# Gate product of the last four token groups as two pairs by Strassen's algorithm, with down weights prepared ahead of up weights

## The chip, the cores and the metric

The kernel runs on one core of a Trainium2 chip. The core has TensorE (PE, matrix products into PSUM), VectorE (DVE), ScalarE (ACT), GpSimd (POOL) and SyncE (SP), which here issues nearly all DMAs. Each engine works through its own instructions in order, and they meet in semaphores. The metric is the device time of one execution in microseconds (us), the median over several runs.

## The reference, cut to what matters

An attention over a context of 128 tokens adds to x (2 x 2048 tokens, 512 wide). A feed-forward block with simulated quantisation follows:

```python
x = act_qdq(x)                                  # 16 bit, one scale for the whole tensor
up = act_qdq(x @ lpbq_dequant(w_up).T)          # weights: 4 bit in blocks of 32; 512 -> 1536
gate = act_qdq(x @ lpbq_dequant(w_gate).T)
sig = fixed_qdq_u16(jax.nn.sigmoid(gate))
gate = act_qdq(gate * sig)
o = act_qdq(gate * up)
return o @ lpbq_dequant(w_down).T               # 1536 -> 512
# act_qdq(x): scale = max(max|x| / 32767, 1e-12); clip(round(x / scale), -32768, 32767) * scale
```

Each `act_qdq` needs the maximum over all 4096 tokens before its first value can be rounded, so the gate product must be finished, and kept somewhere, before any of it is used.

## The kernel before, in words

The 4096 tokens are eight groups of 512 (`NG`), the 1536 inner columns twelve blocks of 128 in six units of two (`UPG`), so a product has 48 units (`NU`). An integer activation and a weight are each held as the sum of two 16-bit floats, high and low; one product of a 128-block by 512 tokens takes three matmuls (high x high, low x high, high x low) for each of four blocks of the inner dimension. One unit of one group is thus 2 x 4 x 3 = 24 matmuls of 128x128 by 128x512.

The stages, in time: attention and normalisation (to 130 us), gate product (130 to 380), up product (380 to 631), down product (631 to the end).

Gate stage. TensorE (`unit`, `product`, `gate`, L864 to L886) writes two PSUM banks per unit, two units ahead of ScalarE. ScalarE (`take_gate`, L1114 on) copies a unit to one of two buffers `gate_out`, and writes its signs; it may refill a buffer when its DMA has landed (`g_st`). VectorE (`gate_max`, L1474) takes the maximum. SyncE (`park_gate`, L424) stores the unit and its signs in HBM (`gate_park`, `sign_park`), and in groups 0 to 2 turns the integer activations of the next groups by DMA transpose (`turn_half`); VectorE splits them (`split_h`). The last six units (from `STAY` = 42) stay in SBUF.

The up and down weights are prepared beside this. VectorE takes block maxima (`block_max`, `block_scales`), GpSimd an all-reduce over the partitions (`all_max`), VectorE the common power of two (`common_scale`), GpSimd quantises in eight passes of four operations (`quant_weights`, L685), ScalarE and VectorE split them (`natural_hi`, `natural_lo`), and SyncE turns them by DMA transpose. Up weights are done in groups 0 to 4, down weights in groups 4 to 6; the turned down weights are parked in HBM (`wd_d`, L448). SyncE then issues the first reloads of gate tiles (`fetch_gate`) to the shelf, a region of 23 places in SBUF, tiles 6 to 14 of the order of use before the last gate unit is through, and 15 to 22 just after.

Up stage. TensorE (`raise_unit`, L897) has eight banks, four units: unit n + 4 starts when ScalarE has taken unit n (`take_up`, L1150, the eviction L993). ScalarE's program is, for n = 0 to 47: the gate tiles of `steps(n)` (three for every two units: integer L1168, absolute value L1173, sigmoid L1181), then `take_up(n)`. VectorE works on the same tiles (L1518, L1523, L1529) and takes the maximum of the up unit (L1511). `take_up(n)` waits until the store of unit n - 2 has landed (`u_st`), as there are two buffers:

```python
if n < STAY:
    need(act, u_mx, n - 1)
    need(act, u_st[n % 2], 8 * (n - n % 2))
```

SyncE's program is one list in order: the shelf's loads, then for each n the first loads of the bench (16 more places, in the room of the split activations as TensorE gives them back), `park_up(n - 1)`, the stores of products of tiles 23 on (`park_product`) and the reloads into their places (`refill`). Up to eight `fetch_gate` are in flight: load k waits for load k - 8. From unit 33 the products are quantised (`settle`).

Down stage. The up tiles come back, are multiplied and quantised, and are multiplied with `WD` (`first_pass`, `down_whole`, `down_split`, L910 to L977).

## Time and profile before

| | us |
|---|---|
| median of 3 runs | 904.1 (903.08 to 907.88) |
| span of the profiled execution | 898.3 |
| busy in it: PE, DVE, ACT, POOL | 865.5, 651.1, 560.2, 157.4 |
| gate matmuls (L871), busy | 250.5, 1152 matmuls |
| up matmuls (L903), busy | 249.0, 1152 matmuls |
| mean granted TensorE clock | 0.994 |

The profile is one execution recorded on the chip. Its span goes from the first to the last instruction; the measured time also holds what lies around it. A group of instructions stands by its source line, engine and operation, with its busy time and the mean of one, and the idle time of the engine ahead of it with what ended that. Matmuls overlap, so a matmul's mean (381 ns) is longer than the step from one to the next. "SPq" is SyncE's DMA queue; the time there is that of issuing, and the time to landing is given apart. "issue" stands for time in which an engine waited for nothing that the profile shows.

### The profile page before, as it was taken

To read this page: it belongs to the slowest core of one execution; us is meant where nothing else is said; L and a number is where in the kernel's file an instruction comes from. 1 tells how busy PE (TensorE), PEld (TensorE's weight loads), DVE (VectorE), ACT (ScalarE), POOL (GpSimd) and SP (SyncE) were. 2 spreads that over 40 slices of the span, in tenths; PEclk is the share of its full clock that TensorE was granted. 3 is DMA by queue.
4 is the path that set the end of the run, shared out by engine and by line. 5 is a ranking of instruction groups with operands and counts; after the bars stand their busy time and mean duration, and the time that the engine had idled before them with its cause. 6 is when DMAs were issued, how large, how long until landed. Compare 5 with 4: busy or idle time off the path is not lost.

```text
span 898.3 us, 11791 instructions
## 1 busy us (share of the span) xinstructions
PE 865.5 (96%) x4144; PEld 426.7 (47%) x4144; DVE 651.1 (72%) x918; ACT 560.2 (62%) x673; POOL 157.4 (18%) x160
## 2 busy tenths in 40 slices
PE   7999969999999999999999989999799989999998
PEld 5777544444444444444444434444344434444443
DVE  4879883754346243279997859856999997999892
ACT  2378875553553454489997859763789975555430
POOL 0099940089001950000000000000000000000000
PEclk9999989999999999999999999999999999999999
DMA  9822319775369649884339993799998897989872
GB/s 347 332 93 98 128 59 305 205 194 198 140 234 296 206 161 294 322 319 157 132 149 327 363 347 142 251 402 373 374 379 265 276 322 271 386 286 406 317 294 100
DMA packets 107548, 230.20 MB, mean 256 GB/s; under 512 B 47216, under 2 KB 47216, under 8 KB 105328
## 3 DMA queue, kind: packets, MB, share of 16 engines
q1 hardware_dynamic: 106352, 225.48, 70.8%
q10 hardware_dynamic: 1152, 4.19, 1.3%
q8 instruction: 21, 0.34, 0.2%
q14 instruction: 23, 0.19, 0.1%
HBM read 127.40 MB, written 92.27 MB: 245 GB/s over the span
## 4 chain that ended last, share of the span: by engine, by line
PE 66%; DVE 16%; issue 8%; DMA 6%; ACT 3%; SPq 0%; POOL 0%; DVEq 0%; ACTq 0%
PE ps L871 28%; PE ps L948 13%; PE ps L903 10%; PE ps L975 3%; DVE big L1596 3%; PE ps L804 3%; DVE big L1589 3%; PE ps L743 2%; PE ps L818 2%; DVE small L1523 2%; DMA big<-gate_park 2%; DMA product_park<-big 2%; DVE small L1511 2%; DVE big L1518 1%; PE ps L965 1%
## 5 line engine op out<-in xcount | busy, mean ns | idle before, releaser
L993 ACT ACTIVATE big<-ps 128x1024 f32<-128x1024 f32 (+2 forms) x166 | 138.7, 845 | 189.6 <-PE ps L871 102.8
L871 PE MATMUL ps<-big 128*128 (+1 forms) x1152 | 250.5, 381 | 2.3 <-DVE big L1460 2.3
L903 PE MATMUL ps<-big 128*128 (+1 forms) x1152 | 249.0, 379 | 2.3 <-ACT big L993 2.3
L871 PEld LDWEIGHTS ps<-big 128*128 128x128 f16 x1152 | 113.1, 98 | 139.4 <-issue 4.6
L903 PEld LDWEIGHTS ps<-big 128*128 128x128 f16 x1152 | 112.6, 98 | 138.5 <-issue 2.8
L1478 DVE TENSOR_REDUCE small<-big 128x1 f32<-128x1024 f32 x48 | 58.3, 1219 | 135.2 <-ACT big L993 135.1
L948 PE MATMUL ps<-big 128*128 128x512 f16 x576 | 125.1, 379 | 2.7 <-DVE big L1617 2.7
L683 POOL PARTITION_ALL_REDUCE small<-small x8 | 3.3, 410 | 509.3 <-DVE small L1558 181.5
L948 PEld LDWEIGHTS ps<-big 128*128 128x128 f16 x576 | 56.2, 98 | 71.1 <-issue 2.9
L929 PE MATMUL ps<-big 128*128 128x512 f16 x384 | 85.2, 383 | 4.5 <-ACT big L1223 4.5
L1529 DVE CUSTOM_DVE_ANT_0 big<-big,small 128x1024 f32<-128x1024 int16 x48 | 61.7, 1284 | 7.3 <-ACT big L1173 0.5
L1252 ACT ACTIVATE big<-big,small 128x1024 int16<-128x1024 f32 x48 | 53.2, 1136 | 16.7 <-DMA big<-up_park 16.5
L929 PEld LDWEIGHTS ps<-big 128*128 128x128 f16 x384 | 37.4, 99 | 52.0 <-issue 5.5
L1511 DVE TENSOR_REDUCE small<-big 128x1 f32<-128x1024 f32 x48 | 58.0, 1214 | 3.4 <-ACT big L993 3.4
L1258 ACT ACTIVATE big<-big 128x1024 f16<-128x1024 int16 x24 | 25.3, 1055 | 53.0 <-DVE big L1611 53.0
L1181 ACT ACTIVATE big<-big,small 128x1024 f32<-128x1024 int16 x48 | 55.1, 1149 | 4.6 <-ACT big L1173 0.4
L1173 ACT ACTIVATE big<-big,small 128x1024 int16<-128x1024 f32 x48 | 54.5, 1136 | 2.4 <-DMA big<-gate_park 2.4
L1216 ACT ACTIVATE big<-big,small 128x1024 int16<-128x1024 f32 x48 | 52.3, 1135 | 5.7 <-DVE small L1444 2.9
L1138 ACT ACTIVATE big<-big 128x1024 int16<-128x1024 f32 x48 | 50.5, 1052 | 6.9 <-DMA sign_park<-big 5.9
L743 PE MATMUL ps<-small,big 128*128 128x128 f32 x248 | 37.9, 294 | 12.8 <-DVE big L1389 5.1
L743 PEld LDWEIGHTS ps<-small,big 128*128 128x128 f32 x248 | 32.2, 153 | 28.6 <-issue 18.4
L691 POOL TENSOR_TENSOR big<-big,small 128x768 f32<-128x768 f32 x24 | 36.5, 1521 | 22.0 <-issue 21.6
(101 smaller groups left out, 1008.9 us busy)
## 6 DMA issues: line engine op xcount, KB each, us to landing
big<-up_park SPq DMA_DIRECT2D x90, 512.0 KB, 6.5
up_park<-big SPq DMA_DIRECT2D x48, 512.0 KB, 3.9
gate_park<-big SPq DMA_DIRECT2D x42, 512.0 KB, 2.9
big<-gate_park SPq DMA_DIRECT2D x42, 512.0 KB, 5.7
sign_park<-big SPq DMA_DIRECT2D x48, 256.0 KB, 3.1
big<-in_x_dram SPq DMA_DIRECT2D x8, 1024.0 KB, 17.5
x_park<-big SPq DMA_DIRECT2D x8, 1024.0 KB, 3.9
product_park<-big SPq DMA_DIRECT2D x16, 512.0 KB, 5.8
```

The costliest lines, as they stand in the source:

```text
L743: return nc.tensor.transpose(dst, src, ident)
L871: mm = nc.tensor.matmul(ps[:, 2 * (n % 2) + j], w[:, a, k, o:o + P], XT[:, g, b, k], start=(k == 0 and a + b == 0), stop=(k == KC - 1 and ...
L903: mm = nc.tensor.matmul(ps[:, b + j], WU[:, a, k, o:o + P], XT[:, g, c, k], start=(k == 0 and a + c == 0), stop=(k == KC - 1 and c == 1))
L929: mm = nc.tensor.matmul(ps[:, b0 + i], halves[:, PART[t], c * 512 + i * P:c * 512 + i * P + P], WD[:, b, 2 * n + c], start=(n == 0 and c + ...
L948: mm = nc.tensor.matmul(ps[:, i], o, WD[:, b, 2 * n + c], start=(n == 0 and c + a + b == 0), stop=(n == UPG - 1 and c + a == 2))
L993: return nc.scalar.activation(dst, src, ACT.Copy)
L1173: nc.scalar.activation(g_abs[:, i % 2], place(i), ACT.Abs, scale=col["ginv"]).then_inc(abs_d, 1)
L1181: nc.scalar.activation(place(i), g_int[:, i % 2], ACT.Sigmoid, scale=col["gsc"]).then_inc(sig_d, 1)
L1252: nc.scalar.activation(r_int[:, m % 4], ring(m), ACT.Copy, scale=col["uinv"]).then_inc(uq_d, 1)
L1478: nc.vector.tensor_reduce(gcol[:, bass.ds(g * UPG + n, 1)], shelf[:, SHELF[n]] if kept else gate_out[:, n % 2], AX.X, ALU.max, apply_absol ...
L1511: nc.vector.tensor_reduce(ucol[:, n:n + 1], up_place(n), AX.X, ALU.max, apply_absolute_value=True).then_inc(u_mx, 1)
L1529: nc.vector.tensor_tensor_reduce(place(i), g_abs[:, s], s_int[:, s], 1.0, scol[:, s:s + 1], ALU.mult, ALU.max, scol[:, s:s + 1]).then_inc( ...
```

## The change

- Groups 0 to 3 keep the old product (24 flat units). Groups 4 to 7 are two pairs. In a pair, the two groups are the rows and two halves of the inner dimension the columns of a 2 x 2 block matrix of tokens; the weights of two output blocks are the other. Seven products (`six`, six matmuls each) replace the eight of a unit in two groups (48 matmuls); 12 such quads are 504 matmuls in place of 576.
- GpSimd forms the four weight sums (ten additions over 1536 elements) and, for each pair, four token sums (ten over 1024), and ScalarE and VectorE split each into high and low.
- The results are put together by ScalarE copies (`copy_out`) and VectorE additions (`combine`) in halves of 512 columns, with their own maxima, signs and stores.
- Down weights are prepared first. They are quantised in flat units 8 to 17, turned in units 16 to 19 and parked in units 17 to 20. Up weights are read twice (block maxima at unit 12, the values at unit 20), quantised behind the first pair's sums and turned in quads 8 to 10. Reads of up and down weights are now in pieces of 128 floats or 256 half-floats, and `WD` is laid out by output block, so that a moving operand is four runs of 128.
- The weight sums lie on the shelf's places 4 to 9, and the early up weights and the second set of token sums on others. Of the six last gate tiles only two (`STAND` = 46) stay in SBUF; the other four and tiles 6 to 22 are fetched after the last gate product.

```diff
@@ SyncE, gate stage @@
             sp.wait_ge(wt_lo, OC)
-            sp.dma_start(WN.rearrange("p (c d) -> p c d", c=OC),
-                         wu_in.rearrange("(c p) d -> p c d", p=P)).then_inc(wn_ld[1], 16)
+            sp.dma_start(WN.rearrange("p (h n) -> p h n", h=KC),
+                         wd_in.rearrange("(h p) n -> p h n", p=P)).then_inc(wn_ld[2], 16)
...
+            def turn_down_weights(h):
+                s, n = (KC - 1 - h) % 2, (KC - 1 - h) // 2
+                if n:
+                    sp.wait_ge(down_st[s], DOWN_ST[s] + 32 * n)
+                for l in range(2):
+                    sp.dma_start(wd_turn[s][:, l], W_DOWN[:, h, l], transpose=True).then_inc(down_turned[s], 16)
+
+            def park_down_weights(h):
+                wd_p = wd_d.rearrange("p (l h c n) -> p l h c n", l=2, h=KC, c=OC)
+                s, n = (KC - 1 - h) % 2, (KC - 1 - h) // 2
+                sp.wait_ge(down_turned[s], DOWN_TURNED[s] + 32 * n + 32)
+                for l in range(2):
+                    sp.dma_start(wd_p[:, l, h], wd_turn[s][:, l]).then_inc(down_st[s], 16)
...
+            for u in range(FLAT):
+                if u == 12:
+                    sp.wait_ge(hq_d, KC + NG - 1)
+                    for k in range(KC):
+                        sp.dma_start(up_early.rearrange("p (k c d) -> p k c d", k=KC, c=OC)[:, k],
+                                     wu_in[:, k * P:(k + 1) * P].rearrange("(c p) d -> p c d", p=P)).then_inc(up_pre, 16)
+                sp.wait_ge(g_ev, u + 1)
+                sp.dma_start(gate_d[u], gate_out[:, u % 2]).then_inc(g_st[u % 2], 16)
+                sp.wait_ge(sign_ev, u + 1)
+                sp.dma_start(sign_d[u], sign_out[:, u % 2]).then_inc(sign_st[u % 2], 16)
+                if u < 2 * (NG - 1):
+                    turn_half(u)
+                if 16 <= u < 20:
+                    sp.wait_ge(wt_lo, OC + 3 * (u - 15))
+                    turn_down_weights(19 - u)
+                if 17 <= u < 21:
+                    park_down_weights(20 - u)
+                if u == 20:
+                    for k in range(KC):
+                        sp.dma_start(WN.rearrange("p (k c d) -> p k c d", k=KC, c=OC)[:, k],
+                                     wu_in[:, k * P:(k + 1) * P].rearrange("(c p) d -> p c d", p=P)).then_inc(wn_ld[1], 16)
...
+            sp.wait_ge(q_mm, Q_MM + 7 * QUADS)
+            for x in (1, 3):
+                sp.wait_ge(c_st[x], C_ST + 16 * stored_halves(x))
+            for i in range(4):
+                fetch_gate(i)
+            for x in (2, 3):
+                park_half(QUADS - 1, x)
             for s in range(2):
-                sp.wait_ge(g_st[s], 16 * STAY // 2)
+                sp.wait_ge(g_st[s], 16 * FLAT // 2)
             for i in range(6, 9):
                 fetch_gate(i)
...
-            for i in range(9, 12):
+            for i in range(9, 16):
                 fetch_gate(i)
...
+            sp.wait_ge(wu_turned, 16 * 2 * KC)
+            for i in range(16, 21):
                 fetch_gate(i)
@@ GpSimd @@
+            weight_sums()
+            all_max(2, "wmx2", "wall2")
             pool.wait_ge(w_blk, 2)
+            for k in range(8):
+                quant_weights(k, 7 - k, 8, binv, bscl)
+            side_sum(0)
+            down_sum(0)
+            all_max(3, "wmx1", "wall1")
+            three_sum(0, 2)
+            four_sum(0, 3)
+            side_sum(1)
+            down_sum(1)
             pool.wait_ge(w_blk, 3)
+            pool.wait_ge(wn_ld[1], 16 * KC)
+            for k in range(2):
+                quant_weights(k, k, 16, up_inv_b, up_scl_b)
+            three_sum(1, 6)
+            for k in range(2, 4):
+                quant_weights(k, k, 16, up_inv_b, up_scl_b)
+            four_sum(1, 7)
+            for k in range(4, 8):
+                quant_weights(k, k, 16, up_inv_b, up_scl_b)
@@ TensorE @@
+            def six(bank, n, w, x, begin):
+                for k in range(2):
+                    for a, b in ((0, 0), (1, 0), (0, 1)):
+                        mm = nc.tensor.matmul(ps[:, bank], w[:, a, k, n * P:(n + 1) * P], x[:, b, k],
+                                              start=(begin and k + a + b == 0), stop=(k + b == 2), skip_group_check=True)
+                mm.then_inc(q_mm, 1)
...
+            def quad(q):
+                base, pr, n = 4 * ((q + 1) % 2), q // UPG, q % UPG
+                g, T = FLAT_G + 2 * pr, turns(pr)
+                need(pe, c_ev, C_EV + 4 * (q - 1) if q > 1 else 0)
+                if q == 1:
+                    pe.wait_ge(g_ev, FLAT)
+                six(base, n, WG[:, 0], XT[:, g, :, 0:2], True)
+                if n == 0:
+                    pe.wait_ge(s_lo, S_LO + 4)
+                    pe.wait_ge(t_lo, T_LO + 4 * pr + 1)
+                six(base + 3, n, SUMS[:, 0], T[:, 0], True)
+                if n == 0:
+                    pe.wait_ge(t_lo, T_LO + 4 * pr + 4)
+                six(base + 2, n, WG[:, 2], T[:, 3], True)
+                pe.wait_ge(c_ev, C_EV + 4 * q + 1)
+                six(base, n, SUMS[:, 1], T[:, 2], False)
+                pe.wait_ge(copy_ev, COPY_EV + 4 * q + 2)
+                six(base + 3, n, SUMS[:, 2], XT[:, g + 1, :, 2:4], False)
+                if q == 0:
+                    pe.wait_ge(g_ev, FLAT - 1)
+                if q + 1 < QUADS:
+                    first_of(q + 1, 4 - base)
+                pe.wait_ge(copy_ev, COPY_EV + 4 * q + 4)
+                six(base, n, SUMS[:, 3], T[:, 1], False)
@@ ScalarE, flat units @@
+            for u in range(FLAT):
+                act.wait_ge(g_mm, u + 1)
+                need(act, g_mx, u - 1)
+                if u >= 2:
+                    act.wait_ge(g_st[u % 2], 16 * (u // 2))
+                copy(gate_out[:, u % 2], ps[:, 2 * (u % 2):2 * (u % 2) + 2].rearrange("p b w -> p (b w)")).then_inc(g_ev, 1)
+                if u % 2 and u < 2 * NG - 3:
+                    h_int((u + 3) // 2)
+                if u in (4, 6, 8, 10):
+                    sum_hi(u // 2 - 2)
+                if 15 <= u < 19:
+                    for c in range(3):
+                        down_hi_weights(OC - 1 - 3 * (u - 15) - c)
+                if 20 <= u < 24:
+                    turn_hi(u - 19, 0, u - 20)
...
@@ VectorE, flat units @@
+                if u in (4, 6, 8, 10):
+                    sum_lo(u // 2 - 2)
+                if u == 7:
+                    block_scales(2)
+                if u == 8:
+                    common_scale(2, 2)
...
+                if u == 20:
+                    block_scales(1)
+                if u == 22:
+                    common_scale(1, 3)
+                if 20 <= u < 24:
+                    turn_lo(u - 19, 0, u - 20)
```

The second pair's sums are split in quads 0 to 3 (`turn_hi(q + 5, 1, q)`, `turn_lo`). `turn_hi` of a pair's j-th sum waits for GpSimd's sum, and for j = 2 of the first pair also until the down weights are parked.

## Rows read from the trace of the kernel before

**Rows 1.** Windows: us, PE, PEld, DVE, ACT, POOL busy (count), clock, DMA share, GB/s.
```profile
130.00:134.00 4.00, 3.86 (x11) 1.53 (x12) 3.90 (x10) 4.00 (x5) 0.00 (x0) 0.59 0.00 0
...
470.00:500.00 30.00, 30.00 (x140) 13.59 (x139) 23.26 (x34) 23.34 (x23) 0.00 (x0) 1.00 0.94 337
500.00:540.00 40.00, 37.71 (x175) 16.93 (x174) 26.97 (x38) 27.92 (x27) 0.00 (x0) 1.00 0.96 347
```
**Rows 2.** Groups of instructions, whole span: the gate and the up matmuls.
```profile
L871 PE MATMUL ps<-big 128*128 (+1 forms) x1152 | 250.5, 381 | 2.3 <-DVE big L1460 2.3
L903 PE MATMUL ps<-big 128*128 (+1 forms) x1152 | 249.0, 379 | 2.3 <-ACT big L993 2.3
```
**Rows 3.** Timeline (start, us, engine, line): first and last gate eviction, a maximum.
```profile
137.21 1.02 ACT L993 ACTIVATE big<-ps 128x1024 f32<-128x1024 f32 x1 [1.88 <-PE ps L871]
...
376.54 1.22 DVE L1478 TENSOR_REDUCE small<-big 128x1 f32<-128x1024 f32 x1 [1.22 <-ACT big L993]
...
380.47 19.80 PE L903 MATMUL ps<-big 128*128 128x512 f16 x91
380.67 1.02 ACT L993 ACTIVATE big<-ps 128x1024 f32<-128x1024 f32 x1 [3.07 <-PE ps L871]
```
**Rows 4.** Timeline of GpSimd around all-reduces, and the VectorE scales between.
```profile
127.25 0.38 POOL L683 PARTITION_ALL_REDUCE small<-small  x1 [5.78 <-issue]
175.88 0.35 POOL L683 PARTITION_ALL_REDUCE small<-small  x1 [48.25 <-DVE small L1312]
176.84 0.32 DVE L1324 TENSOR_SCALAR small<-small 128x192 f32<-128x192 f32 x1
183.05 1.47 POOL L691 TENSOR_TENSOR big<-big,small 128x768 f32<-128x768 f32 x1 [6.82 <-issue]
...
225.20 1.48 POOL L697 TENSOR_TENSOR big<-big,small 128x768 f32<-128x768 f32 x1
```
**Rows 5.** Groups by form: 0 to 130 us, and GpSimd's additions 130 to 381.
```profile
L993 ACT ACTIVATE big<-ps 128x512 f32<-128x512 f32 x56 | 32.7, 596 | 38.9 <-PE ps L743 21.7 <-PE ps L780 5.7 <-PE ps L761 5.7
...
L1361 DVE SCALAR_TENSOR_TENSOR big<-ps,small,big 128x512 f32<-128x512 f32 x32 | 23.9, 746 | 6.8 <-PE ps L818 6.5
...
L691 POOL TENSOR_TENSOR big<-big,small 128x768 f32<-128x768 f32 x16 | 24.7, 1541 | 14.6 <-issue 14.6
```
**Rows 6.** SyncE's queue: the load when gate weights are done; a transpose pair.
```profile
135.00 0.41 SPq L403 DMA_DIRECT2D big<-in_L_ffn_w_up_dram  x1
...
277.24 4.40 SPq L407 DMA_TRANSPOSE big<-big  x2
```
**Rows 7.** DMAs, median us to landing: issued 262 to 264, then 336 to 356.
```profile
gate_park<-big SPq DMA_DIRECT2D x1, 512.0 KB, 9.7
...
gate_park<-big SPq DMA_DIRECT2D x4, 512.0 KB, 3.4
...
big<-big SPq DMA_TRANSPOSE x7, 4.8
```
**Rows 8.** Timeline of ScalarE in the up stage.
```profile
384.62 1.15 ACT L1168 ACTIVATE big<-big,small 128x1024 int16<-128x1024 f32 x1 [1.84 <-DVE small L1444]
...
401.21 1.01 ACT L993 ACTIVATE big<-ps 128x1024 f32<-128x1024 f32 x1
...
531.54 1.15 ACT L1168 ACTIVATE big<-big,small 128x1024 int16<-128x1024 f32 x1 [7.11 <-DMA big<-gate_park]
...
537.16 1.01 ACT L993 ACTIVATE big<-ps 128x1024 f32<-128x1024 f32 x1
...
598.16 1.03 ACT L993 ACTIVATE big<-ps 128x1024 f32<-128x1024 f32 x1 [7.24 <-DMA up_park<-big]
```
**Rows 9.** SyncE's queue after the gate product, and the window 388 to 392.
```profile
383.24 4.13 SPq L452 DMA_DIRECT2D big<-gate_park  x8
392.54 22.91 SPq L504 DMA_DIRECT2D up_park<-big  x6
...
388.00:392.00 4.00, 4.00 (x20) 1.86 (x19) 2.49 (x4) 3.90 (x5) 0.00 (x0) 1.00 1.00 411
```

593 lines of the change are left out of this document (399 added, 194 removed).

## The prediction

> **What bounds the kernel now.** I read the busy time by stretch first. In the gate and up stages TensorE is busy without a gap but for 2.3 us near 538 us [rows 1, 2]. So TensorE sets both stages, and its instruction count is their length: 1152 matmuls each, at 5.18 us per unit of 24. That pace is (380.67 - 137.21) / 47 for the eviction copies of units 0 to 47, and 0.216 us for one matmul [rows 3]. The gate product ends at T = 380.5.
>
> Next I followed ScalarE through the up stage. It is a chain of its own. It starts when the gate scale is known (384.62), takes up unit 2 at 401.21, which is T + 20.7, and runs without idle until about 463. It reaches unit 26 at 537.16 after a 7.11 us wait for a parked gate [rows 8]. TensorE may run four units ahead of these copies; its only gap, 2.3 us, was spent waiting for that copy [rows 2]. From 470 to 540 ScalarE is busy 51.3 of 70 us and the DMA engines are full at 337 to 347 GB/s [rows 1]. So in the up stage the chain ScalarE, product store, reload is as late as TensorE: what delays it against T by more than a fraction of a microsecond comes back as a TensorE gap.
>
> **Part 1: the matmuls removed.** A quad (one unit of two groups) is 7 products of 6 matmuls in place of 48. Twelve quads save 72 matmuls: 72 x 0.216 = 15.5 us off the gate stage. Inside a quad evictions become four ScalarE copies (0.60 us, like the 128x512 copies), four signs, four VectorE combines (0.75 us, like L1361) and four maxima, some 5 us on each engine in 9.1 us [rows 5]. The first combine is due 3.9 us into the quad and done after three combines, about 2.6 us. Cost 0. The flat part runs at the old pace until unit 23 ends at 256.2; the quads' third and fourth products then want the four token sums.
>
> **Part 2: GpSimd's new queue.** An all-reduce and ordinary work don't follow each other freely. The all-reduce at 175.88 released VectorE's scales, done at 177.16, and the first quantising step started at 183.05, 5.9 us later, charged to issue. The other way, the all-reduce at 127.25 had 5.78 us of issue in front [rows 4]. Before, nobody waited for either. Now: the weight sums start when the gate weights are done at 135.0 [rows 6], plus 5.9, so 141. Ten additions over 1536 elements at 1.54 us per 768 [rows 5] are 31 us, ending near 172 (the last three wait for VectorE in unit 4). Then 5.8 us, the all-reduce at 178, the scales after unit 8 at 182, 5.9 us: quantising starts at 188 where it was 183. The eight passes took 43.6 us (183.05 to 226.7 [rows 4]) and end at 231. Six additions over 1024 elements (2.1 us each) end at 244. Then 5.8 us, the all-reduce near 250, 5.9 us, and the third sum starts at 256 and ends at 260. Its high half, low half, the fourth sum (4.2) and again both halves (1.1 and 1.3 us) bring the last low half to 269. The product that wants it would start at 256.2 + 3.9 = 260.1. Wait by this path: 9 us.
>
> The f16 inputs are a form that no row has; 1.54 us per 768 is f32. The Trainium skill, GPSIMD Engine Reference, section 3.1, gives tensor_tensor over 2048 f32 elements as 4497 ns, which makes 2.25 us of one addition here where the row makes 2.1. By the page the fourth sum of the second pair would be about 3 us later; the trace's row decides.
>
> **Part 3: SyncE's new queue.** The down weights are turned in units 16 to 19, two transposes each, and now also parked; the turn of block h waits until block h + 2 has landed in HBM. SyncE holds 4.4 us for a pair of such transposes [rows 6], a transpose lands 4.8 us after issue and a store among transposes 3.4 us after [rows 7]. From sign 16 at 222.6: pair 226 (quick, the queue is empty), sign 17 and pair 234, two stores 235, wait 238.4, pair 242.8, stores, gate and sign 18/19 244.7, wait 247.1, pair 251.5, stores 252.4, gate 20 at 252.8, wait for the last transpose 254, stores 255, four loads of up weights 256.6, gate 21 at 257. That store stands behind 3 MB: a gate store issued 2.9 us after such a load landed 9.7 us later, 12.6 after the load's issue [rows 7]. So it lands near 268.5; the copy of unit 23 needs its buffer (269.5), then high half 270.6 and low half 271.9. Wait by this path: 11.8 us. The two paths are near each other, so if one is shorter the other still holds. I take 12.5, bounds 8 and 17, above the second path because these loads come in 512-byte pieces, which no row shows (from 0 to 5 us on 3 MB).
>
> The Trainium skill (DMA: Bandwidth & Descriptors, Specifications) puts full rate at pieces of 512 B and more, by which this wait would be 11.8.
>
> After such a gap TensorE starts slow: 130 to 134 us has 11 matmuls in 4 us at a granted clock of 0.59, the 1.2 GHz level for most of it [rows 1]. Eight matmuls at double time: +1.7.
>
> **Part 4: rest of the gate stage.** Second pair: GpSimd does six additions, two passes (5 us each), a sum, two passes, a sum: its fourth sum is due in quad 3 near 304 and ready near 308; ScalarE has 3.3 us of slack there. +1 (0 to 5). Eight up-weight transposes in quads 8 to 10 hold SyncE 17.6 us in which it also issues about 20 half stores; their buffers are wanted one quad later. +1.5 (0 to 4). They land before the up product starts. Sum for the gate stage: -15.5 + 12.5 + 1.7 + 1 + 1.5 = +1.2, so T = 381.7. The scale after T waits for two combines and two maxima (2.9 us) in place of a copy and a maximum (1.02 + 1.22 [rows 3]): +0.5, hidden by the next part.
>
> **Part 5: gate tiles fetched after T.** This is the main term. Before, 9 of the 17 shelf loads were issued before T, eight at 383.24 to 387.4, and up unit 0 was parked at 392.54 [rows 9]. Now the Strassen sums and the up weights lie on the shelf, so 21 loads (i = 0 to 3, 6 to 22) are issued after T, all ahead of that store on SyncE, and load k waits for load k - 8. 21 x 0.524 MB plus 0.65 MB of halves and signs at the 0.41 MB/us of 388 to 392 us [rows 9] is 28.4 us, from T + 0.7 with 1.3 for the start and 1 for the landing: T + 31.5. The store of up unit 0 goes out at T + 22 and lands behind them, T + 33. ScalarE's copy of unit 2 needs its buffer: T + 33.2 for T + 20.7. Everything on ScalarE behind it (gates 5 on) and VectorE behind that moves by 12.5 us. TensorE gaps: unit 6 waits 3 us, and the gap at unit 30 grows by the other 9.5, as nothing between 401 and 537 is released by TensorE: the product stores and reloads follow ScalarE. +12.5 (bounds 6 and 15), and +1.5 for the clock after the long gap. 14.0.
>
> **Part 6: down stage.** Down weights come back in 512-byte pieces and the moving operand reads four runs of 128 columns: no row for either. I take 0; bounds 0 and 5 us (a fraction of a nanosecond to 3 ns on some 1152 matmuls, or 3 MB slower). The copy of unit 38 already waits 7.24 us for a store [rows 8]; this moves with the chain.
>
> **Sum.** 898.3 + 1.2 + 14.0 = 913.5 for the profiled span. The span lies 5.8 us below the median 904.1, so 919.3 us; I say 919.
>
> **Rivals.**
> (a) The up stage absorbs the late stores: the 18.7 us that ScalarE idles from 470 to 540 [rows 1] are due to queueing of product stores, and the delay shrinks there. For it: idle time exists and the DMA engines rest from 400 to 460. Against: each wait ends with a reload that follows ScalarE's own product. Decisive point: unit 26's copy less than 4 us later against T. Then 904.1 + 1.2 + 3 = 908, or 905 if nothing is left: not slower. Chance 0.14.
> (b) The gate stage keeps its gain: sums and turned weights are ready by 260, no wait at the first pair. It needs both GpSimd without the 5.9 us steps and SyncE 11 us earlier. T = 366 to 369, the up stage loses 14: 902 to 906. Chance 0.12.
> (c) Faster: (a) and (b) together, place the first quad and up unit 2, price -15.5 + 2.5 + 1, 890 to 894. It decides if the first quad starts by 262 and the first up store lands by T + 22. Chance 0.05, and 0.04 for partial mixes of (a) and (b) under 899.6.
> (d) 512-byte pieces run at half rate: the early load of up weights in unit 12 holds the gate stores and stops units 14 to 16 for 5 us, the load at unit 20 adds 5, the down weights 3: 925 to 932. Chance 0.08.
> The change does cut TensorE's instructions as it says; I give no chance to the opposite.
>
> **Chances.** Forecast 0.57 (911 to 926), with a, b, c, d as above. A measurement here can tell 0.5% (4.5 us) from no change: faster 0.09 (c and mixes), same 0.24 (a and b but for their edges), slower 0.67. Range 904 to 929: it holds the forecast, most of (a), half of (b) and half of (d).
>
> **What would show it.** Gate matmuls 1080 in place of 1152. TensorE idle of 8 to 17 us between its third and fourth product after unit 23, released by VectorE's low half; GpSimd's first step after each all-reduce 5.9 us after its release; an SP queue in which gate store 21 lands 10 us or more after issue. Up unit 2's copy waiting for the up store until about T + 33, unit 26's copy near T + 169, and a TensorE gap over 8 us near unit 30. If the up copy isn't late, or T lies under 372, the prediction is wrong at that part.

## The result and the profile after

The changed kernel takes 933.8 us (median of 4 runs, 932.7 to 936.9) against 903.6 us of the kernel before on the same chip: a ratio of 1.033, 95% interval 1.030 to 1.037. That is 30 us slower where 15 were forecast (919 us), and 5 us above the end of the range (929). The direction was right, the size was not.

The first view is TensorE's timeline of the changed kernel through the gate stage (L1078 is a flat unit, L1094 a Strassen product) and the up stage (L1148). Columns: start, length, engine, line, operation, tiles, count, and in brackets the idle time before with what ended it. It answers [rows 2], where each stage was one block.

```profile
130.95 83.07 PE L1078 MATMUL ps<-big 128*128 128x512 f16 x384 [0.23 <-DVE big L1767]
216.28 22.58 PE L1078 MATMUL ps<-big 128*128 x96 [2.27 <-ACT big L1243]
239.28 5.35 PE L1078 MATMUL ps<-big 128*128 x24 [0.41 <-ACT big L1243]
247.13 17.37 PE L1078 MATMUL ps<-big 128*128 x72 [2.50 <-ACT big L1243]
264.33 4.05 PE L1094 MATMUL ps<-big 128*128 128x512 f16 x18
282.77 40.32 PE L1094 MATMUL ps<-big 128*128 128x512 f16 x174 [14.39 <-DVE big L1790]
328.29 20.33 PE L1094 MATMUL ps<-big 128*128 128x512 f16 x84 [5.19 <-DVE big L1830]
349.37 49.38 PE L1094 MATMUL ps<-big 128*128 128x512 f16 x228 [0.75 <-DVE big L1830]
398.59 31.24 PE L1148 MATMUL ps<-big 128*128 128x512 f16 x144
433.74 105.46 PE L1148 MATMUL ps<-big 128*128 128x512 f16 x480 [3.90 <-ACT big L1243]
540.02 10.53 PE L1148 MATMUL ps<-big 128*128 x48 [0.83 <-ACT big L1243]
552.14 10.53 PE L1148 MATMUL ps<-big 128*128 x48 [1.58 <-ACT big L1243]
570.31 95.60 PE L1148 MATMUL ps<-big 128*128 x432 [7.64 <-ACT big L1243]
```

The gate product ends at T = 398.6 (380.5 before): +18.1 us, forecast +1.2. The up product then lasts 267.3 us (398.6 to 665.9) against 251.2 before (380.5 to 631.7): +16.1, forecast +14.0. The down stage, from the up product's end to the end of the span, is 266.6 us before and 266.7 after. So one term carries nearly all of the error: the gate stage.

The gate stage can be added up from these lines. At 0.2166 us for a matmul, the pace of the last block (49.38 / 228), 1080 matmuls are 233.9 us. Above that the changed kernel has: a start 0.8 us later; 8.6 us in the flat units (264.33 - 130.95 for 576 x 0.2166 = 124.8), of which 5.2 are gaps and the rest slower matmuls behind them, 1.8 behind each of the two longer ones; the wait of 14.4 us in the first pair, where 12.5 were forecast; 2.6 us in the 174 matmuls behind it (40.32 for 37.7); and for the second pair 5.2 and 0.75 us of gaps and 2.1 of slow matmuls. Together 34.5, less 0.9 that the stage before also had above its pace: 33.6 - 15.6 = 18.0 us.

The granted clock by stretch (busy TensorE with its count, then the clock; with the DMA share and GB/s last) shows what a gap can cost beyond its idle time. Two rows of the changed kernel, then the same ten microseconds of e1, a kernel with the same code up to T:

```profile
150.00:214.00 64.00, 64.00 (x297) 1.00 0.86 233
214.00:224.00 10.00, 7.73 (x29) 0.83 0.96 291
```

```profile
214.00:224.00 10.00, 8.68 (x41) 1.00 0.88 285
```

After 2.3 us idle the ten microseconds of the changed kernel hold 29 matmuls where 46 fit at full clock: 3.7 us lost, 1.4 of them beyond the gap, as the clock was at the 1.2 GHz level for part of the stretch (0.50 from 217 to 219). In e1 a gap of 2.2 us at the same place left the clock at 1.00 and cost nothing more, and so did its later gap of 2.5 us. So this price of a short gap is there in one execution and not in another; what decides it was not found.

### The profile page after: what moved, and what is told of

The parts are those of the page before. It is cut to its first block, busy times and chain, and to the rows that moved or that the text cites. A ratio compares the mean times of both kernels' runs of the same rounds, so it can differ in the third digit from the quotient of the medians.

```text
span 932.6 us, 11991 instructions
## 1 busy us (share of the span) xinstructions
PE 864.2 (93%) x4072; PEld 423.7 (45%) x4072; DVE 723.3 (78%) x1012; ACT 578.8 (62%) x733; POOL 242.5 (26%) x190
## 3 DMA queue, kind: packets, MB, share of 16 engines
q10 hardware_dynamic: 1152, 4.19, 1.2%
## 4 chain that ended last, share of the span: by engine, by line
PE 49%; POOL 14%; DMA 10%; DVE 10%; issue 8%; ACT 5%; SPq 4%; ACTq 0%; DVEq 0%; POOLq 0%
PE ps L1148 19%; PE ps L1198 13%; PE ps L1078 7%; PE ps L1094 6%; PE ps L1225 3%; DMA big<-gate_park 2%; POOL big L898 2%; DMA big<-in_L_ffn_w_gate_dram 2%; DVE big L1703 2%; DMA up_park<-big 2%; POOL big L826 2%; POOL big L820 2%; POOL big L814 2%; ACT big L1516 1%; DVE big L1964 1%
## 5 line engine op out<-in xcount | busy, mean ns | idle before, releaser
L1148 PE MATMUL ps<-big 128*128 (+1 forms) x1152 | 253.4, 383 | 13.9 <-ACT big L1243 13.9
L1243 ACT ACTIVATE big<-ps 128x1024 f32<-128x1024 f32 (+2 forms) x142 | 113.9, 814 | 137.0 <-DMA up_park<-big 28.7
L1148 PEld LDWEIGHTS ps<-big 128*128 128x128 f16 x1152 | 113.3, 99 | 153.8 <-issue 13.6
L1078 PE MATMUL ps<-big 128*128 (+1 forms) x576 | 128.4, 386 | 5.4 <-ACT big L1243 5.2
L1094 PE MATMUL ps<-big 128*128 128x512 f16 x504 | 114.1, 390 | 20.3 <-DVE big L1790 14.4
L1198 PE MATMUL ps<-big 128*128 128x512 f16 x576 | 125.2, 379 | 2.4 <-DVE big L1985 2.4
L1078 PEld LDWEIGHTS ps<-big 128*128 128x128 f16 x576 | 56.8, 99 | 76.8 <-ACT big L1243 6.6
L1179 PE MATMUL ps<-big 128*128 128x512 f16 x384 | 85.0, 384 | 5.1 <-ACT big L1523 5.1
L1094 PEld LDWEIGHTS ps<-big 128*128 128x128 f16 x504 | 50.2, 100 | 84.0 <-DVE big L1790 14.9
L1198 PEld LDWEIGHTS ps<-big 128*128 128x128 f16 x576 | 56.1, 98 | 70.9 <-issue 3.7
L1879 DVE TENSOR_REDUCE small<-big 128x1 f32<-128x1024 f32 x48 | 58.1, 1215 | 16.3 <-ACT big L1243 16.3
L1552 ACT ACTIVATE big<-big,small 128x1024 int16<-128x1024 f32 x48 | 53.4, 1137 | 18.8 <-DMA big<-up_park 18.6
L1179 PEld LDWEIGHTS ps<-big 128*128 128x128 f16 x384 | 37.5, 99 | 52.3 <-issue 5.6
L1795 DVE TENSOR_REDUCE small<-big 128x1 f32<-128x1024 f32 x24 | 29.2, 1217 | 37.4 <-ACT big L1243 37.1
L826 POOL TENSOR_TENSOR big<-big 128x1024 f32<-128x1024 f32 (+3 forms) x18 | 46.6, 2589 | 25.1 <-DVE big L1784 7.5
L1830 DVE TENSOR_TENSOR big<-ps,big 128x512 f32<-128x512 f32 x48 | 31.2, 683 | 26.5 <-PE ps L1094 26.4
```

The lines of the kernel that those rows point to most:

```text
L826: nc.gpsimd.tensor_tensor(dst, a, b, op).then_inc(plink, 1)
L1078: mm = nc.tensor.matmul(ps[:, 2 * (n % 2) + j], WG[:, x, a, k % 2, o:o + P], XT[:, g, b, k], start=(k == 0 and a + b == 0), stop=(k == KC ...
L1094: mm = nc.tensor.matmul(ps[:, bank], w[:, a, k, n * P:(n + 1) * P], x[:, b, k], start=(begin and k + a + b == 0), stop=(k + b == 2), skip_ ...
L1148: mm = nc.tensor.matmul(ps[:, b + j], WU[:, a, k, o:o + P], XT[:, g, c, k], start=(k == 0 and a + c == 0), stop=(k == KC - 1 and c == 1))
L1179: mm = nc.tensor.matmul(bank_of(b0 + i), halves[:, PART[t], c * 512 + i * P:c * 512 + i * P + P], WD[:, b, :, 2 * n + c], start=(n == 0 an ...
L1198: mm = nc.tensor.matmul(bank_of(i), o, WD[:, b, :, 2 * n + c], start=(n == 0 and c + a + b == 0), stop=(n == UPG - 1 and c + a == 2))
```

## Experiments

Each kernel ran beside the kernel before on the same chip. All but e10 are slower than it with the whole interval. "T" is the end of the gate product. Times are medians; T, waits and gaps are those of one profiled execution per kernel. How far such a reading can move by itself shows in e1, whose code is that of the changed kernel up to T: its T is 397.2 for 398.6, its flat units take 131.4 us for 133.4, and its first wait is 18.0 us for 14.4. A microsecond or two of T, and a few of one wait, are therefore no effect.

### e1: the first up stores between the gate loads

```diff
-            for i in range(9, 16): fetch_gate(i)
-            ...   (waits, then loads 16 to 22)
+            for i in range(9, 11): fetch_gate(i)
             ...
                 if n:
                     park_up(n - 1)
+                if 1 <= n < 7:
+                    fetch_shelf(9 + 2 * n)
+                    fetch_shelf(10 + 2 * n)
```

> The changed kernel with one edit after T: the first up stores go out between the gate loads (loads 0 to 10, store of unit 0, loads 11 and 12, store of unit 1, loads 13 and 14, and so on) instead of behind all 21 loads. Theory that the late first store makes the up stage long: ScalarE's copy of unit 2 starts at T + 20 to T + 24 (it was T + 34.1), the copy of unit 26 is earlier by as much, the 7.6 us TensorE gap near unit 30 and most of the 3.9 us gap near unit 6 go, and the up stage is 8 to 14 us shorter: 920 to 926 us. Rival that the stage is long because the 21 loads load the DMA engines, whatever the order: the copy of unit 2 moves but unit 26's comes no earlier against T, and the time stays at 931 to 936. Rival that later product stores absorb half: 926 to 930.

Measured: 922.8 us, ratio 1.023 (1.019 to 1.027), against 1.033 (1.030 to 1.037). The up product lasts 256.2 us (397.2 to 653.4), 11.1 less. Here are SyncE's queue in the changed kernel and ScalarE's copy of up unit 2 in it (timelines as above), then the same two in e1:

```profile
408.55 12.65 SPq L571 DMA_DIRECT2D big<-gate_park  x14
421.26 12.78 SPq L624 DMA_DIRECT2D up_park<-big  x3
```

```profile
432.66 1.02 ACT L1243 ACTIVATE big<-ps 128x1024 f32<-128x1024 f32 x1 [12.83 <-DMA up_park<-big]
```

```profile
409.55 0.34 SPq L626 DMA_DIRECT2D up_park<-big  x1
```

```profile
418.22 1.00 ACT L1248 ACTIVATE big<-ps 128x1024 f32<-128x1024 f32 x1
```

The store of unit 0 leaves at T + 22.7 in the one and T + 12.3 in the other; the copy of unit 2 comes at T + 34.1 (forecast T + 33.2) and T + 21.0 (T + 20.7 before). ScalarE's late wait for a parked gate, the place at which the delay comes back, ends at T + 165.0 in the changed kernel, T + 153.7 in e1 and T + 151.0 before [rows 8]; the copy of unit 26, 5.6 us behind it, comes at T + 170.6 in the changed kernel (forecast T + 169). The wait in the changed kernel and in e1:

```profile
563.54 1.15 ACT L1467 ACTIVATE big<-big,small 128x1024 int16<-128x1024 f32 x1 [7.71 <-DMA big<-gate_park]
```

```profile
550.90 1.15 ACT L1472 ACTIVATE big<-big,small 128x1024 int16<-128x1024 f32 x1 [7.81 <-DMA big<-gate_park]
```

The wait itself has not shrunk (7.7 and 7.8 us): it follows the chain, as forecast, and rival (a) of the prediction, that the idle time absorbs the delay, falls. Two thirds of the up stage's loss is the order of SyncE's queue; 5 us remain (256.2 for 251.2). TensorE in e1 shows where they lie:

```profile
397.23 155.56 PE L1153 MATMUL ps<-big 128*128 128x512 f16 x720
557.67 95.77 PE L1153 MATMUL ps<-big 128*128 x432 [4.88 <-ACT big L1248]
```

The gap near unit 6 is gone, the one at unit 30 is 4.9 us (7.6 in the changed kernel, 2.3 before), so it went only in part, and the 432 matmuls behind it take 95.8 us where they took 93.4 before. Why ScalarE is still 2.7 us late at its wait wasn't isolated.

### e2: the up weights in whole rows

```diff
-  up_early...(k c d)[:, k] <- wu_in[:, k * P:(k + 1) * P]   (512-byte pieces)
+  up_early...(k c d)[:, k] <- wu_in[k * 384:(k + 1) * 384]  (2 KB pieces)
   (the same for the second read)
```

> The changed kernel with both reads of the up weights (3 MB each, beside unit 12 and beside unit 20) in pieces of 2 KB in place of 512 bytes: the same bytes, loads and places, but the weights arrive in another order, so that part of the result is another product. Theory that the 512-byte pieces hold SyncE and the gate stores: the four loads of unit 12 hold SyncE for under 4 us (7.4 before), the 2.3 us TensorE gap near unit 14 goes, store 21 leaves some 4 us earlier, T is 3 to 7 us earlier, 927 to 931 us. Rival that 3 MB delay the stores whatever their pieces, or that GpSimd's sums hold the first pair anyway: T within 2 us of the changed kernel's, 932 to 936 us.

Measured: 932.9 us, ratio 1.036 (1.032 to 1.040): no gain. T is 396.2, but its gate stage began 0.9 us earlier. SyncE's hold on the early read, in the changed kernel and in e2:

```profile
200.17 7.38 SPq L514 DMA_DIRECT2D big<-in_L_ffn_w_up_dram  x4
207.59 2.64 SPq L517 DMA_DIRECT2D gate_park<-big  x1
```

```profile
199.25 2.70 SPq L514 DMA_DIRECT2D big<-in_L_ffn_w_up_dram  x4
202.00 0.54 SPq L517 DMA_DIRECT2D gate_park<-big  x1
```

So 512-byte pieces do cost: 4.7 us of SyncE for 3 MB and 2.1 us more on the next store; the gap near unit 14 falls from 2.3 to 0.5 us. But TensorE resumes the first pair at 280.5 for 282.8, after a wait of 16.5 us instead of 14.4: most of what was won ahead of the pair was waited out at it. Both paths to the pair still ended late. Gate store 21 left 6.1 us earlier (265.2 for 271.3), but it still stood behind the 3 MB, and copy 23 got its buffer only 2.4 us earlier (276.9 for 279.3); GpSimd's fourth sum was ready at 277.3. Of rival (d) the stop near unit 14 was there, at 2.3 us and not 5; in the time it came to near nothing. The experiment's own rival, 932 to 936 us, came true. The Trainium skill (DMA: Bandwidth & Descriptors, Specifications) puts full rate at pieces from 512 B on. The median landing, 8.7 us with 512-byte pieces and 8.3 with 2 KB, agrees; that sentence says nothing of the issuing queue, where the difference lay.

### e3, e4, e5: one path or both to the first pair

e3 moves the all-reduce of the up weights on GpSimd behind the sums of both pairs; e4 moves the second read of the up weights behind the stores of unit 23; e5 does both, with a better place for the all-reduce:

```diff
 e3 (GpSimd)                          e4 (SyncE)
-    all_max(3, "wmx1", "wall1")      -    if u == 20:   # read up weights
     three_sum(0, 2)                  +    if u == 23:
     four_sum(0, 3)
     side_sum(1)                      e5: e4's edit, and on GpSimd
     down_sum(1)                          ... down_sum(1)
+    all_max(3, "wmx1", "wall1")          all_max(3); three_sum(1, 6)
     (two passes, three_sum, ...)         four_sum(1, 7); then eight passes
```

> The changed kernel with the all-reduce for the up weights moved on GpSimd from between the second and third token sum to behind all the sums that the first pair needs (and the scale that follows it moved into quad 1). Theory of two near paths: GpSimd's fourth sum is ready near 265 instead of 279.5, but TensorE still waits for gate copy 23 and the low half behind it, which the late gate store holds: the first gap shrinks by 0 to 2 us only, 932 to 935 us. Rival that GpSimd's path alone holds the first pair: the gap shrinks by 7 to 14 us, 920 to 927 us. The second pair's sums come a little later or as before; its 5.2 us gap stays.

> The changed kernel with the second read of the up weights (3 MB) issued behind the stores of unit 23 in place of behind unit 20, so that no gate store of the flat part stands behind it. Theory of two near paths: gate store 21 lands by 266 and copies 22 and 23 come at once, but TensorE still waits for GpSimd's fourth sum (279.5) and its halves: the first gap shrinks by 0 to 2 us, 932 to 935 us. Rival that SyncE's path alone holds the first pair: the gap shrinks by 8 to 12 us, 922 to 926 us. Rival that the up weights now come too late for their quantising (needed near 294): the second gap grows and the time is 935 to 940 us.

> The changed kernel with both paths to the first pair shortened: the second read of the up weights behind the stores of unit 23, and on GpSimd the order third sum, fourth sum, first two sums of the second pair, all-reduce, third and fourth sum of the second pair, then all eight passes over the up weights (their halves one quad later). Theory of two near paths: TensorE resumes the first pair near 273 instead of 281 to 283 (gap 5 to 8 us for 14.4), the second gap (5.2 us) goes, T is 10 to 17 us earlier, and the up stage stays as long as in the changed kernel: 914 to 922 us, where each edit alone brought nothing. Rival that something else holds the first pair at 281 (the down weights' stores, ScalarE's own queue): T within 5 us of the changed kernel's, 926 to 934 us. Rival that the passes for the up weights now come too late and the gap reappears in quads 5 to 9: 920 to 928 us.

Measured: e3 947.0 us, ratio 1.050 (1.046 to 1.054), 12 us above its forecast of 932 to 935; e4 932.9 us, 1.037 (1.032 to 1.042), as forecast; e5 930.6 us, 1.031 (1.026 to 1.037), where 914 to 922 were forecast. The two paths in the changed kernel, first GpSimd, then SyncE and ScalarE:

```profile
260.51 0.83 POOL L805 PARTITION_ALL_REDUCE small<-small  x1 [6.75 <-issue]
268.43 2.11 POOL L826 TENSOR_TENSOR big<-big 128x1024 f32<-128x1024 f32 x1 [7.09 <-issue]
...
277.36 2.12 POOL L888 TENSOR_TENSOR big<-big 128x1024 f32<-128x1024 f32 x1
```

```profile
263.25 7.97 SPq L529 DMA_DIRECT2D big<-in_L_ffn_w_up_dram  x4
271.26 3.18 SPq L517 DMA_DIRECT2D gate_park<-big  x1
```

The fourth sum is ready at 279.5. Gate store 21, behind the 3 MB, leaves at 271.3 to 274.4, copy 23 waits for it until 279.3, and the high and the low half end at 282.7: both paths end within a microsecond, as forecast. In e4 the store path is gone (copy 23 at 273.1), and ScalarE's high half waits for GpSimd's fourth sum; in e3 GpSimd has the fourth sum at 277.9, not near 265, and copy 23 waits for the store. The line of e4, then two of e3:

```profile
277.94 1.06 ACT L1344 ACTIVATE big<-big 128x1024 f16<-128x1024 f32 x1 [3.83 <-POOL big L888]
```

```profile
265.16 2.12 POOL L826 TENSOR_TENSOR big<-big 128x1024 f32<-128x1024 f32 x1 [12.17 <-DVE big L1790]
```

```profile
284.11 1.02 ACT L1243 ACTIVATE big<-ps 128x1024 f32<-128x1024 f32 x1 [10.96 <-DMA gate_park<-big]
```

The middle line says why e3's sum is late. The third sum is built on the second in one buffer (`raw_sum[:, 1]`), and so is the fourth on the third; each has to wait until VectorE has made the low half of the sum before. Those halves stand on ScalarE and VectorE behind gate copies that wait for their stores (copy 21 for 4.5 us in e3 and 4.6 in e4), and the third sum's high half waits for the parked down weights (2.8 us in e3). So without its all-reduce GpSimd is still led by SyncE: it gains 3 us on its third sum (265.2 for 268.4; 260.5 in e5) and stands idle for the rest. The two paths are not independent of each other.

Neither edit alone shortens the wait (14.1 us in e3 and 15.3 in e4, for 14.4); both together cut it to 8.2, TensorE resuming at 275.8. The theory of two near paths holds for the first pair, with that link between them. The time does not follow it: e5's T is 393.2, where 382 to 389 were forecast. The edit has a price of its own. The first two sums of the second pair now stand ahead of an all-reduce with 7.0 and 7.1 us of issue on its two sides, the third sum starts at 302.8, and ScalarE, which works in order, stands in quad 2 until it has it:

```profile
311.29 37.94 PE L1090 MATMUL ps<-big 128*128 128x512 f16 x168 [2.92 <-DVE big L1824]
...
359.80 18.30 PE L1090 MATMUL ps<-big 128*128 128x512 f16 x84 [1.08 <-DVE big L1824]
379.26 9.24 PE L1090 MATMUL ps<-big 128*128 128x512 f16 x42 [1.16 <-DVE big L1824]
```

e3 pays the same in full: gaps of 7.9, 2.6 and 1.5 us in its second pair. They are most of its 12 us in T; the rest lies in its flat units, which take 139.2 us for 133.4 though the edit changes nothing there. VectorE's twelve low halves of the down weights take 22.4 us in it for 18.8 (e8 is about them); why they met GpSimd's work worse is not shown. An all-reduce among ordinary work takes GpSimd away for about 14 us, before the first pair or before the second.

### e6: no token sums

The sums on GpSimd, their halves on ScalarE and VectorE, and TensorE's waits for them are left out, with e4's edit; the products take the tokens themselves, so the gate is another product.

```diff
-    six(base + 3, n, SUMS[:, 0], T[:, 0], True)
+    six(base + 3, n, SUMS[:, 0], XT[:, g, :, 0:2], True)
     (the other three likewise; side_sum, down_sum, three_sum,
      four_sum, turn_hi and turn_lo left out)
```

> The changed kernel without token sums: GpSimd's sums, ScalarE's high halves and VectorE's low halves of them are left out, and the products take the tokens themselves in their place (so the gate is another product); the second read of the up weights is behind the stores of unit 23. It measures what the gate stage is worth when neither path exists. Theory that the token sums and the late gate store make both gaps: first gap 3 to 8 us (copy 23 still waits for store 21), no second gap, T 379 to 385, 912 to 920 us. Rival that TensorE's pace in the quads is itself limited by the copies and combines: gaps of 1 us or more in most quads, T over 388, 922 us or more.

Measured: 919.4 us, ratio 1.019 (1.013 to 1.025), T = 382.0, waits of 3.8 and 3.0 us in the first two quads and none behind: the last 438 matmuls are one block of 96.6 us. The quads keep their pace when the copies and combines are all that ScalarE and VectorE do; forecast cost 0 of part 1 stands. Time and T came as forecast. Even so T is no better than before. The 1080 matmuls at full pace would end at 364.2; the flat units, untouched by this edit, take 6.2 us more than that (gaps of 2.4, 0.5, 1.3 and 1.5 us), the two waits 6.9, and slower matmuls in the quads 4.8.

### e8: short passes on GpSimd

Each pass over the down weights takes one block of 24, so most down weights are not quantised.

```diff
     for k in range(8):
-        quant_weights(k, 7 - k, 8, binv, bscl)
+        quant_weights(k, 7 - k, 8, binv, bscl, 1)   # first block alone
```

> The changed kernel with GpSimd's eight passes over the down weights cut to one block of 24 each (so the down weights are mostly not quantised): GpSimd is quiet while VectorE makes the low halves in units 15 to 18. Theory that VectorE's low halves are slow beside GpSimd's passes and hold ScalarE and TensorE: they take 0.68 us each (1.1 to 2.3 before), ScalarE's waits for them and TensorE's gaps of 0.4 and 2.5 us in units 15 to 18 go, the 2.3 us gap near unit 14 stays, unit 23 ends 3 to 5 us earlier; the first pair is then held by SyncE alone, near 277: 926 to 931 us. Rival that the low halves are slow for another reason (their form or their places): still 1.1 us or more each, the gaps stay, 932 to 935 us.

Measured: 926.9 us (two runs), ratio 1.026 (1.019 to 1.034), as forecast. The gaps of units 15 to 18 are gone: 192 matmuls are one block of 43.3 us, and the last flat unit ends 5.2 us earlier (259.2 for 264.3; against e1's flat units it is 3.2). e11 below, with the same edit on e7, gains 5.1. The first pair then waits for SyncE alone, as forecast: copy 23 gets its buffer at 275.2, and TensorE resumes at 278.7. VectorE's low halves of the down weights, three a unit, in the changed kernel and then in e8:

```profile
223.64 4.42 DVE L1703 TENSOR_TENSOR big<-big 128x512 f16<-128x512 f32 x3
...
229.11 3.29 DVE L1703 TENSOR_TENSOR big<-big 128x512 f16<-128x512 f32 x3
```

```profile
221.92 1.89 DVE L1705 TENSOR_TENSOR big<-big 128x512 f16<-128x512 f32 x3
```

The lengths of single ones (minimum, median and maximum in ns, with first and last start) for all 24 in the kernel before, for the twelve of the down weights in the changed kernel, and for those in e8:

```profile
L1396 DVE TENSOR_TENSOR big<-big x24: 680/683/694, 232.6 to 342.6; 128x512 f16<-128x512 f32 x24
```

```profile
L1703 DVE TENSOR_TENSOR big<-big x12: 832/1306/2607, 223.6 to 246.9; 128x512 f16<-128x512 f32 x12
```

```profile
L1705 DVE TENSOR_TENSOR big<-big x12: 681/685/693, 221.9 to 237.1; 128x512 f16<-128x512 f32 x12
```

The same operation takes 0.83 to 2.61 us, 1.31 in the median of twelve, while GpSimd works, and 0.68 to 0.69 when it is quiet. The changed kernel shows the other half of it by itself: the low halves of the up weights take 0.86 to 1.88 us until GpSimd's last pass ends at 345.5, and 0.68 to 0.69 from then on. ScalarE's next high half waits for such a low half, since both overwrite the weights in place, and its eviction of the gate unit stands behind three of them. The Trainium skill (SBUF — State Buffer, "SBUF: two separate sides") gives the reason: a VectorE operation with two SBUF inputs and a GpSimd operation that reads SBUF exclude each other. The traces read here agree. The combines take one operand from PSUM and kept 0.68 us beside GpSimd; that agrees too. The prediction did not use this rule, though the change moves exactly such work: before, the twelve low halves of one matrix were made from 232.6 to 259.8 and the twelve of the other from 327.5 on, between and behind GpSimd's passes (they end at 226.7 [rows 4] and at 326.8), and took 0.68 us each.

### e7, e9, e10, e11: all edits, and what still holds them

e7 joins e1, e5, and the early read of the up weights spread over units 12 to 15. e9 leaves out SyncE's eight transposes of the down weights, e11 shortens the passes as in e8, e10 does both.

```diff
 e7, early read                      e9, on top of e7
-    if u == 12:                     -    turn_down_weights: two transposes
-        for k in range(KC):         +    left out; park_down_weights
+    if 12 <= u < 16:                +    stores W_DOWN[:, h, l] as it lies
+        for k in (u - 12,):
```

> All edits together: up stores between the gate loads (the first experiment's edit), both paths to the first pair shortened (the edits of both paths together), and the early read of the up weights spread over units 12 to 15, one quarter a unit. If the losses of the gate stage and the up stage add, as the theory has it: 900 to 909 us, 24 to 34 below the changed kernel and within 1% of the kernel before. Rival that the gains don't add (the up stage's chain takes back what the gate stage gives): 912 to 922 us.

> The kernel of all edits together (e7_all, T = 389.8 us, 917.1 us, 9.5 us gap at the first pair) with SyncE's eight transposes of the down weights left out; they are parked as they lie (so the down product is another one). Theory that after the edits GpSimd's chain of sums (second sum 252.8, third 260.5, fourth 267.3, its halves 269.7) stands only a little behind SyncE's: the gap at the first pair shrinks by 2 to 5 us, T 385 to 388, 912 to 916 us. Rival that SyncE's queue alone holds it by now: the gap shrinks by 7 us or more, 905 to 910 us.

> The kernel of all edits together (e7_all) with GpSimd's eight passes over the down weights cut to one block of 24 each, as in the eighth experiment. Theory that the passes cost twice, on GpSimd's own path to the sums and by slowing VectorE's low halves in units 15 to 18: TensorE's gaps there (2.1 and 2.7 us) and the slow clock behind them go, 5 to 6 us, and the first gap shrinks to 2 to 6 us as only SyncE's path is left: T 377 to 383, 904 to 911 us. Rival that only the slowed low halves count and SyncE's path keeps the first gap: T 384 to 386, 911 to 914 us.

> The kernel of all edits together (e7_all) with both left out: the down weights' transposes on SyncE and all but one block in 24 of GpSimd's passes over them. It measures the gate stage when nothing is late for the first pair. Theory (72 matmuls less are worth their 15.5 us once SyncE and GpSimd keep up): no gap over 2 us until the second pair, T 368 to 376, 895 to 904 us. Rival that the quads themselves run with small gaps on ScalarE and VectorE (1 to 2.5 us in six of twelve in e7_all) that remain: T 377 to 382, 904 to 910 us.

| kernel | time, us | ratio to before (95%) | T | last flat unit ends | first wait |
|---|---|---|---|---|---|
| e7 | 917.1 | 1.015 (1.010 to 1.021) | 389.8 | 259.5 | 9.5 |
| e9, no transposes | 915.5 | 1.014 (1.010 to 1.019) | 389.3 | 261.5 | 7.2 |
| e11, short passes | 911.9 | 1.011 (1.007 to 1.015) | 386.5 | 254.4 | 10.4 |
| e10, neither | 903.9 | 1.002 (1.000 to 1.005) | 379.7 | 254.6 | 3.6 |

e7 wins back 17 of the 30 us and leaves out nothing of the reference, yet it is 1.5% slower than before. It missed its own forecast (900 to 909) and lies in its rival's range, though not for the rival's reason: the gains do add (8.8 us of T and 9.7 in the up stage, against 18.1 in the whole span), but the gate stage gave too little, as in e5. The spread read did remove the gap near unit 14: 480 matmuls in one block. e9 fell where forecast (915.5 us, first wait 2.3 us shorter) but for its T. In e11 the rival came true: the first wait did not shrink (10.4 for 9.5 us), T and time are the rival's to within 0.5 us, and only the flat units gained. e11's profiled execution was the fastest of five, 907.2 us.

The four kernels are one more case of two paths. Relieving SyncE alone is worth 0.5 us of T, relieving GpSimd alone 3.3, both 10.1, more than the sum; in the median times it is 1.6, 5.2 and 13.2 us. In e7 and e11 the third sum's high half waits for the parked down weights, in e9 and e10 for GpSimd. In e10 the flat units are one block of 124.5 us, and what remains of the waits is this:

```profile
130.28 124.48 PE L1078 MATMUL ps<-big 128*128 128x512 f16 x576 [0.20 <-DVE big L1766]
254.59 4.05 PE L1094 MATMUL ps<-big 128*128 128x512 f16 x18
262.24 12.22 PE L1094 MATMUL ps<-big 128*128 128x512 f16 x48 [3.60 <-DVE big L1789]
276.15 18.30 PE L1094 MATMUL ps<-big 128*128 128x512 f16 x84 [1.70 <-DVE big L1827]
297.90 37.91 PE L1094 MATMUL ps<-big 128*128 128x512 f16 x168 [3.45 <-DVE big L1827]
```

What still holds the first pair in e10 is the one buffer of the sums. GpSimd is free from 218.4 on and stands idle until VectorE has made the second sum's low half in unit 21:

```profile
247.92 2.13 POOL L830 TENSOR_TENSOR big<-big 128x1024 f32<-128x1024 f32 x1 [29.48 <-DVE big L1789]
```

From there third sum, two halves, fourth sum and two halves follow one another and end at 262.2, 14.3 us later, while TensorE wants the result at 258.6. Neither a quiet GpSimd nor a quiet SyncE shortens that. Earlier halves of the second sum, or a buffer more, would be the thing to try; no run did.

e10's T (379.7) and its small gaps are those of the second forecast, not the first, though the time of 903.9 us lies at the upper end of the first: gaps of 0.3 to 3.5 us stay in six places of the quads (8.3 us in all). With the first wait (3.6) and slower matmuls behind the gaps (some 3.6) they use up the 15.5 us that 72 matmuls save. The one at 297.9 is the moved all-reduce again; the small ones, 0.8 to 1.1 us, lie where ScalarE and VectorE also make the up weights' halves, and e6, which kept those halves in quads 4 to 7 but had no sums, had none of them. Which of e7's two shifts makes them was not separated.

## Why the prediction was right or wrong

**What bounds the kernel.** Right. TensorE sets both stages, and ScalarE's chain carries each delay of the up stage to the gap near unit 30.

**Part 1.** 72 matmuls at 0.216 us: right, the last undisturbed 228 run at 0.2166. Combines and copies at cost 0: right (e6). The sentence that failed is "the flat part runs at the old pace until unit 23 ends at 256.2". It ended at 264.3. (As an end of TensorE's work 256.2 was itself some 1.7 us too late: undisturbed it comes at 254.4 and 254.6, in e11 and e10.) That sentence put the flat units' loss at nothing. VectorE's low halves, 0.68 us each before, were given no price of their own, though the change moves them under GpSimd's passes; they took up to 2.6, and ScalarE and then TensorE waited for them. e8 and e11 put 5 us on this (e8 against e1 3). The rest of the 8.6 is the early read of the up weights, which the prediction had only as rival (d): it stopped TensorE for 2.3 us near unit 14, with slow matmuls behind it, and e7's spread read removed that. Because the down weights' turn begins with these halves, and the units before were late already, SyncE's first transposes also came 9 us late (232.0 where about 223 was worked out), and every time of part 3 moved with them.

**Part 2.** The mechanism was right, one of its rules read at the wrong end. The 5.9 us were counted from the release by VectorE's scale; here the first step came 4.5 us after it (188.5 to 193.0). What stays alike is the time from the all-reduce's own end: 6.8 and 7.8 us before, 7.6 and 7.1 here. Ahead of the one between the sums it was 6.8 us (5.8 worked out). The fourth sum, due about 266 in that part, was ready at 279.5: the passes began 5.0 us late (VectorE's block scales were ready at 184.9, the all-reduce came at 185 for 178), they took 46.2 us for 43, the six additions 14.6 for 13, the all-reduce with what lies around it 14.7 for 12. The additions with two f16 inputs, a form without a row, were no dearer by themselves: 2.2 us per 1024 elements with VectorE idle beside them (from 286.9), up to 2.6 beside its low halves.

**Part 3.** The mechanism was right; the start was 9 us late, the pair of transposes cheaper than taken (3.3 to 3.7 us, not 4.4), and the second read dearer (8.0 us of SyncE and 3.2 for the store behind it, where 1.6 were taken for the four loads). The wait came out as near as 14.4 for 12.5 only because both its ends were late: TensorE began to wait at 268.4, not 260.1, and resumed at 282.8, not 272.6. That is luck in the number. Taking the higher of two near paths was right: with either edit alone (e3, e4) the wait stayed. The slow matmuls behind it cost 2.6 us for 1.7.

**Part 4.** The mechanism was right, the size wrong: 1 us for the second pair, 8.1 measured, above the bound of 5. The fourth sum was due at 308 with ScalarE wanting it near 304; it was ready at 323.9, as its start was 13.5 us late and the work up to it took 44.4 us for 42, while the quads had moved by 10 only. ScalarE works in order and stood before its high half, with no product copied out meanwhile:

```profile
323.95 1.06 ACT L1344 ACTIVATE big<-big 128x1024 f16<-128x1024 f32 x1 [7.99 <-POOL big L888]
```

Of these 8.0 us ScalarE's slack took 2.8 (3.3 worked out), a TensorE gap of 5.2 was left, and another of 0.75 and 2.1 us of slow matmuls, for which the part had no term, came behind it. The bound of 5 was too narrow because it did not carry the lateness of part 2 with it. The transposes in quads 8 to 10 (1.5) cost nothing.

**Part 5.** Right: 14.0 forecast, 16.1 measured, its steps on ScalarE within a microsecond or two (copy of unit 2 at T + 34.1 for 33.2, of unit 26 at T + 170.6 for 169). Inside the sum two errors nearly cancel: TensorE's gaps grew by 11.7 us (12.5 forecast), and the slow matmuls behind them cost over 4 (1.5 forecast). The gap near unit 30 is 7.6 us, where over 8 was named as a sign; 2.4 more lie in two small ones ahead of it.

**Part 6.** Right: 0 forecast, 0.1 us measured for the down stage as a whole, with 512-byte pieces and strided operand in it.

**The time.** The sum for the span was 913.5; 16.9 us more in the gate stage and 2.1 in the up stage make 932.5 (932.6 measured). The 16.9 are, term by term: 8.6 in the flat units, put at 0; 7.1 in the second pair (8.1 for 1); 1.9 in the first wait; 0.9 in the slow matmuls behind it; less the 1.5 for the transposes; and small differences of start and pace. So the step that failed is the first term, the flat part at its old pace, and next to it the price of the second pair.

The distance from the span to the median, 5.8 us in the runs before, was 1.2 here. Elsewhere an execution's time is about 2 us above its own span; the 5.8 came of a profiled execution some 4 us faster than the median. At 5.8 the forecast would have been 4.6 us further off, which is luck again. The range failed because the flat units had no bounds at all and the second pair narrow ones.

## What to carry to other kernels

A duration read from a trace belongs to the neighbourhood in which it was read. When a change moves VectorE work with two SBUF operands under GpSimd work, expect twice its row (1.31 for 0.68 us here, 2.6 at most). When two paths end within a few microseconds, removing one shows nothing; ask also whether one feeds the other through a shared buffer, as the sums did here. In an in-order queue the cost of a late operand is paid by everything behind the wait, not by its consumer alone. A product that saves 72 of 1152 matmuls has to bring its sums, their halves and its reordered loads in under 15.5 us; here the first up store behind 21 loads alone took 11 of them.

## What the runs showed of the hardware

- An all-reduce on GpSimd between ordinary operations, with nothing else to wait for, has 5.7 to 7.6 us of issue ahead of it and 6.7 to 7.9 behind it (the kernel before, the changed one and all eleven others): about 14 us around 0.4 to 1.4 us of work.
- Reading 3 MB in 512-byte pieces holds SyncE for 7.4 us (8.0 the second time), in 2 KB pieces for 2.7 (3.8), with nearly the same landing time (8.7 and 8.3 us); issuing the 512 KB store behind it takes 2.6 (3.2) against 0.5 us.
- VectorE's 128x512 subtraction with two SBUF inputs: 0.68 us beside an idle GpSimd, 0.83 to 2.6 us beside a busy one.
- A TensorE gap of 2.3 us cost 1.4 us more of slow matmuls in the changed kernel (granted clock 0.83), one of 2.2 us at the same place in e1 none (1.00); gaps of 14.4 and 18.0 us cost 2.6 and 2.9 us more (changed kernel, e1).
